# A two-stage attention layer on one core: turned inputs spread over four slots, norm two groups ahead, output row added by VectorE

## What is computed

```python
ln_out = layernorm(hidden_states, ln1_s, ln1_b)
q, k, v = split(ln_out @ w_qkv + b_qkv)
x = hidden_states + merge(attention(q, k, v, ltor_mask)) @ w_ao + b_ao
ln_out = layernorm(x, ln2_s, ln2_b)
q = ln_out @ w_q + b_q
k, v = split(encoder_states @ w_kv + b_kv)
x = x + merge(attention(q, k, v, cross_mask)) @ w_co + b_co
return x + gelu(layernorm(x, ln3_s, ln3_b) @ w1 + b1) @ w2 + b2
# attention: scores * mask - 10000 * (1 - mask), softmax, times v
```

## Time and profile before

| | us |
|---|---|
| runs: median (lowest to highest) | 2038.16 (2036.88 to 2038.91) |
| the profiled execution | 2038.14 |
| its span, first to last instruction | 2036.3 |
| self stage, one group in the loop | about 36.5 |
| cross stage, one group in the loop | about 40.8 |
| MLP, from 1302.8 | 733.5 |

### The profile page before, as it was taken

One profiled execution on the slowest core, in us unless ns is written; L12 is line 12 of the kernel. 1 busy time (PEld: TensorE's weight loads), 2 busy tenths in 40 slices (PEclk: granted clock), 3 DMA queues, 4 the chain that ended last, 5 costly groups with the idle time before them and its releaser, 6 DMA issues. The chain is left out here.

```text
span 2036.3 us, 40263 instructions
## 1 busy us (share of the span) xinstructions
PE 1879.3 (92%) x13328; PEld 1489.4 (73%) x13328; DVE 980.7 (48%) x3338; ACT 1026.6 (50%) x3202; POOL 669.7 (33%) x778
## 2 busy tenths in 40 slices
PE   5999999999988988898889888799999999999999
PEld 4777777777766766676667766588888888888887
DVE  3656566565665556555655565452232323233221
ACT  2666666666666756666666666432222222222222
POOL 2444444444454434344434344440101202020110
PEclk9999999999999999999999999899999999999999
DMA  4311111121121312121112112301010110101010
GB/s 143 106 54 57 44 33 59 41 57 44 33 79 45 112 45 67 44 64 44 61 50 64 44 56 95 135 11 57 6 62 0 62 52 10 52 10 57 5 42 21
DMA packets 71103, 108.07 MB, mean 53 GB/s; under 512 B 12544, under 2 KB 20736, under 8 KB 71040
## 3 DMA queue, kind: packets, MB, share of 16 engines
q1 hardware_dynamic: 71040, 107.27, 16.6%
HBM read 82.07 MB, written 25.17 MB: 53 GB/s over the span
## 5 line engine op out<-in xcount | busy, mean ns | idle before, releaser
L913 POOL TENSOR_TENSOR a_p_s<-a_p_s,a_rcp 128x512 f32<-128x512 f32 x256 | 280.5, 1096 | 679.6 <-DVE a_rcp L759 679.6
L636 ACT ACTIVATE a_p_s<-a_t_s,a_mx 128x128 f32<-128x128 f32 x1024 | 398.8, 395 | 4.9 <-DVE a_mx L750 4.9
L1073 PE MATMUL m_ps_h<-mlp_xT,wt 128*128 128x512 f32 x1536 | 377.3, 396 | 1.8 <-PEq L342 1.8
L1087 PE MATMUL m_ps_y<-m_down_hi,m_g_r 128*128 128x512 f32 x1024 | 343.7, 395 | 0.1
L1073 PEld LDWEIGHTS m_ps_h<-mlp_xT,wt 128*128 128x128 f32 x1536 | 288.0, 188 | 70.9 <-issue 2.0
L1165 DVE TENSOR_TENSOR m_g_r<-m_g_t,m_g_r 128x512 fp32r<-128x512 f32 x128 | 95.3, 745 | 472.8 <-ACT m_g_r L1144 472.8
L740 DVE TENSOR_TENSOR a_ps_s<-a_ps_s,a_m_mul 128x512 f32<-128x512 f32 x256 | 176.7, 690 | 121.6 <-PE a_ps_s L454 119.6
L750 DVE CUSTOM_DVE_ANT_0 a_t_s<-a_ps_s,a_m_add 128x128 f32<-128x128 f32 x1024 | 229.2, 279 | 0.1
L1087 PEld LDWEIGHTS m_ps_y<-m_down_hi,m_g_r 128*128 128x128 f32 x1024 | 192.4, 188 | 44.6 <-issue 0.5
L1128 ACT ACTIVATE m_g_t<-m_ps_h,bias_cols 128x512 f32<-128x512 f32 x128 | 88.1, 689 | 269.5 <-PE m_ps_h L1073 269.3
L496 PE MATMUL a_ps_q<-wt,a_cT 128*128 128x512 f32 x768 | 217.9, 420 | 1.8 <-DVE a_cT L763 1.4
(11 more groups left out here) (78 smaller groups left out, 2544.9 us busy)
## 6 DMA issues: line engine op xcount, KB each, us to landing
a_x_t<-in_x SPq DMA_DIRECT2D x32, 256.0 KB, 2.9
a_res_t<-in_x SPq DMA_DIRECT2D x32, 256.0 KB, 3.1
x_after_self<-a_y_t SPq DMA_DIRECT2D x32, 256.0 KB, 2.0
a_x_t<-x_after_self SPq DMA_DIRECT2D x32, 256.0 KB, 2.8
a_enc_t<-in_ctx SPq DMA_DIRECT2D x32, 256.0 KB, 3.2
a_res_t<-x_after_self SPq DMA_DIRECT2D x32, 256.0 KB, 2.9
raw_wt<-in_w SPq DMA_DIRECT2D x32, 256.0 KB, 4.0
x_after_cross<-a_y_t SPq DMA_DIRECT2D x32, 256.0 KB, 2.0
```

The costliest lines, as they stand in the source:

```text
L636: last = nc.scalar.activation(p_s[:, n % 2, j], t_s[:, n % 2, j], ACT.Exp, scale=-1.0, bias=mx[:, n % 2, j:j + 1], accum_out=sums[:, n % 2 ...
L913: nc.gpsimd.tensor_tensor(p_s[:, n % 2], p_s[:, n % 2], rcp[:, n % 2].unsqueeze(2).to_broadcast([P, HQ, P]), ALU.mult).then_inc(s["normal" ...
L1073: last = nc.tensor.matmul(ps_h[j % 2][:], w1[hw][:, j // KC, kc, (j % KC) * P:(j % KC + 1) * P], xT[:, hx, kc], start=(k == 0), stop=(k == ...
L1087: last = nc.tensor.matmul(ps_y[b][:], g_r[:, j % 2, hg, b * P:(b + 1) * P], w2[hw][:, j // KC, j % KC], start=(j == 0 and x == 0), stop=(j ...
```

## The change

Four things are done.

1. **Turns.** In the cross stage (for groups 17 to 31) TensorE turns x0 in slot 0, x1 and ctx0 in slot 2 and ctx1 in slot 3; between them lie products. For self groups and for group 16 they stay in slots 2 and 3. `flips` lists them for all three engines, those with `last` false ahead of the values' or output's second half. Since `ps_c` is shared, the values of sequence 0 wait for x0's low half.
2. **Norm.** It is made for group g+2 instead of g+1, in slots 5 to 7 instead of 0 to 2: statistics and aggregates in slot 5, centring and first norm in 6, second norm in 7; the inverse roots on GpSimd in slot 5. SP loads x of g+2 in slot 0 instead of 3.
3. **Sums.** In slots 0 and 4 VectorE inverts the sums ahead of scaling the scores; a wait that went with the reciprocal there is kept by a bare semaphore increment, `mask_begun`. GpSimd normalises ahead of preparing the mask.
4. **Output row.** VectorE adds the residual to the output product straight from PSUM, in slots 1 and 4; ScalarE's copy and GpSimd's addition go. TensorE, whose next products use that bank, waits for `y_done` instead of `y_copied`.

```diff
+            def norms_ahead(g):
+                return not isinstance(g, int) or g + 2 <= gN + 1
+
+            def flips(g, n, nxt, last):
+                if not nxt:
+                    at_end = {(gN - 1, 4): (gN, 0), (gN - 1, 5): (gN, 1), (gN, 0): (gN + 1, 0), (gN, 1): (gN + 1, 1)}
+                    return [("x", *at_end[g, n])] if last and (g, n) in at_end else []
+                if not crosses(g + 1):
+                    return [("x", g + 1, n - 2)] if last and n in (2, 3) else []
+                if opens(g + 1):
+                    return [("x", g + 1, n - 2), ("enc", g + 1, n - 2)] if last and n in (2, 3) else []
+                if last:
+                    return [("enc", g + 1, 0)] if n == 2 else []
+                return {0: [("x", g + 1, 0)], 2: [("x", g + 1, 1)], 3: [("enc", g + 1, 1)]}.get(n, [])
...
@@ SP
-                        if n == 3 and (nxt or leads(g + 2 if isinstance(g, int) else 0) and g < gN):
+                        if n == (0 if g != -1 else 2) and norms_ahead(g):
                             load_x(g + 2, 0)
                             load_x(g + 2, 1)
...
@@ TensorE
                         elif known(g, 2):
-                            pe.wait_ge(s["y_copied"], at((g - 1) * GB))
+                            pe.wait_ge(s["y_done"], at((g - 1) * GB))
...
                                 pe.wait_ge(s["k_copied"], at((g + 1) * KC))
+                                if crosses(g) and not (isinstance(g, int) and g == gN - 1):
+                                    pe.wait_ge(s["xTl_done"], at((g + 1) * GB + 1))
...
                         if cur if n >= 3 else prev:
                             weigh_values(*lag(g, n, 3))
+                        for what, k, b in flips(g, n, nxt, False):
+                            (flip_x if what == "x" else flip_enc)(k, b)
                         if n == 0 and prev:
                             outputs(g - 1, 0, 1, cur)
...
@@ ScalarE
-                        if n in (0, 3) and prev:
-                            output_row(g - 1, n // 3)
+                        for what, k, b in flips(g, n, nxt, False):
+                            (flip_x if what == "x" else flip_enc)(k, b)
...
@@ VectorE
+                    def output_row(g, b):
+                        k = g * GB + b + 1
+                        dve.wait_ge(s["res_ready"], at(k))
+                        if known(g, 1):
+                            dve.wait_ge(stored[b], at(16 * g))
+                        dve.wait_ge(s["o_done"], at(k))
+                        nc.vector.tensor_tensor(y_t[:, b], ps_r, res_t[:, b], ALU.add).then_inc(s["y_done"], 1)
...
+                        if n % KC == 0 and (cur if n >= 2 else prev):
+                            invert_sums(*lag(g, n, 2))
                         if cur:
                             scale_scores(g, n)
-                        if n == 2 and ahead:
-                            norm(g + 1, 1)
-                        if n == 0 and ahead:
-                            statistics(g + 1, 0)
-                            statistics(g + 1, 1)
...
+                        if n == 7 and ahead:
+                            norm(g + 2, 1)
+                        if n in (1, 4) and prev:
+                            output_row(g - 1, n // 4)
+                        if n == 5 and ahead:
+                            statistics(g + 2, 0)
+                            statistics(g + 2, 1)
...
+                        if n % KC == 0 and cur and known(g, 1):
+                            dve.wait_ge(s["scaled"], at(slot_no(g, n)))
+                            dve.sem_inc(s["mask_begun"], 1)
+                        if n % KC and (cur if n >= 2 else prev):
...
+                            moments(g + 2, 0)
+                            moments(g + 2, 1)
+                        if n == 6 and ahead:
+                            centre(g + 2, 0)
+                            norm(g + 2, 0)
+                            centre(g + 2, 1)
...
@@ GpSimd
-                    def output_row(g, b):
...
+                        if cur if n >= 2 else prev:
+                            normalise(*lag(g, n, 2))
                         if n == 0 and cur:
                             prepare_mask(g, 1)
                         if n == 7 and nxt:
                             prepare_mask(g + 1, 0)
...
-                        if n == 0 and norms_next(g, cur, nxt):
-                            root(g + 1, 0)
-                            root(g + 1, 1)
+                        if n == 5 and norms_ahead(g):
+                            root(g + 2, 0)
+                            root(g + 2, 1)
...
-                        if n in (1, 4) and prev:
-                            output_row(g - 1, n // 4)
```

More of the change, by code:

```diff
@@ L401, in slot @@
                     def slot(g, n, cur, prev, nxt):
-                        if n == 3 and isinstance(g, int) and g in (NG - 2, gN - 2):
+                        if n == 0 and isinstance(g, int) and g in (NG - 2, gN - 2):
                             for b in range(GB):
@@ L561, in flip_x @@
                         pe.wait_ge(s["xn_done"], at(g * GB + b + 1))
-                        if b == 1 and crosses(g) and not leads(g):
-                            pe.wait_ge(s["encTl_done"], at((g - NG) * GB + b))
-                        elif b == 1 or leads(g) and g > gN:
+                        if b == 1 and opens(g) and crosses(g):
+                            pe.wait_ge(s["encTl_done"], 1)
+                        elif b == 1:
                             pe.wait_ge(s["xTl_done"], at(g * GB + b))
+                        elif leads(g) and g > gN:
+                            pe.wait_ge(s["xTl_done"], g * GB)
+                        elif leads(g) or known(g, 1) and not crosses(g - 1):
+                            pe.wait_ge(s["v_copied"], at((g - 1) * GB + 1))
                         elif known(g, 1):
+                            pe.wait_ge(s["k_copied"], at(g * KC))
+                        if b == 1 and known(g, 1) and crosses(g - 1) and not leads(g):
                             pe.wait_ge(s["v_copied"], at((g - 1) * GB + 1))
@@ L571, in flip_enc @@
                         pe.wait_ge(enc_in[b], at(16 * (g - NG + 1)))
-                        pe.wait_ge(s["xTl_done"], at(g * GB + b + 1))
+                        if opens(g):
+                            pe.wait_ge(s["xTl_done"], g * GB + b + 1)
+                        elif b == 0:
+                            pe.wait_ge(s["xTl_done"], at(g * GB + GB))
+                        else:
+                            pe.wait_ge(s["encTl_done"], at((g - NG) * GB + b))
                         flip(enc_t, b, "encT_done")
@@ L595, in slot @@
                             bias_products(g)
-                        if n in (2, 3) and nxt:
-                            flip_x(g + 1, n - 2)
-                            if crosses(g + 1):
-                                flip_enc(g + 1, n - 2)
+                        for what, k, b in flips(g, n, nxt, True):
+                            (flip_x if what == "x" else flip_enc)(k, b)
                         if n == 3 and cur:
@@ L712, in slot @@
                             split_weights(g, n)
-                        if n in (2, 3) and nxt:
-                            flip_x(g + 1, n - 2)
-                            if crosses(g + 1):
-                                flip_enc(g + 1, n - 2)
+                        for what, k, b in flips(g, n, nxt, True):
+                            (flip_x if what == "x" else flip_enc)(k, b)
                         if not (cur or prev) and n >= 4:
                             split_weights(g, n)
-                        if n in (0, 1, 4, 5) and leads(g):
-                            flip_x(g + n // 4, n % 4)
                     def split_weights(g, n):
@@ L746, in mask_scores @@
                         b, c = divmod(n, KC)
-                        if not known(g, 1) and n < 2:
+                        if not known(g, 1) and (n < 2 or c == 0):
                             dve.wait_ge(s["scaled"], at(slot_no(g, n)))
@@ L826, in slot @@
                             mask_scores(g, n)
[L827 removed]
+                        if n == 5 and ahead:
                             if not cur:
[L829 to L835 removed]
+                                dve.wait_ge(s["stats_done"], (g + 2) * GB + 2)
+                            moments(g + 2, 0)
[4 more added lines that the diff above has]
+                            centre(g + 2, 1)
                         if n == 2 and prev:
```

42 lines of the change are left out of this document (9 added, 33 removed).

## The result

The changed kernel takes 1924.23 us (median of 4 runs, 1923.62 to 1924.77) against 2038.16: ratio 0.9442 [0.9425, 0.9458], 113.9 us less. The profiled execution's span is 1922.6, 113.7 less than before.

A forecast was written before the change was run, and what follows sets the result against it. TensorE, busy 92% of the span, was taken as the bound, so only its waits pay. Self loop 14.0, cross loop 57.8, odd groups and end 19.6 sum to 91.4 us: 2038.1 to 1947, range 1937 to 1982.

The forecast's parts named there:

- Part 1: Cross groups, turns spread over four slots: removes 3.85 us a group, with 0.1 a group taken for a late ctx0 turn.
- Part 2: Norm two groups ahead, sums inverted first: removes 1.17 us a group; new waits 0 in self, 0.1 in cross.
- the chain of 959.3: Slots 6 and 7: estimated sequence from mask and centring through norms and scaling, its normalisation ending at 959.3.
- the shift by 0.4: Slots 5 to 7: output row and four small GpSimd ops delay the normalisation's end by 0.4, to 959.7.
- the forecast's 4.82: Gain per looped cross group, in us: 3.85 from turns plus 1.17 from GpSimd waits, less 0.2 of new waits.
- Part 3: Output row on VectorE, slots 1 and 4: removed copies and additions all off the path, added ops covered; nothing.
- rival B: Cross groups: spread turns not covered, ScalarE stands in exponents; 1.5 a group in 15 groups, 1970 us, chance 0.12.
- The odd groups: Groups 0, 1, 14 to 17, 30 and the end, outside the loops: together 19.6 us won.
- A: Slots 5 to 7: norm's burst collides, TensorE waits for GpSimd there; 1.25 us x 28 groups, 1982 us, chance 0.16.
- C: Slots 5 to 7: collision at its bound plus slow-clocked TensorE, 3.6 a group; slower overall, 2051 us, chance 0.04.
- D: Cross groups: added waits before values hold the spread in step; 3 of 5 us lost each, 1992 us, chance 0.03.
- E: Whole change: every new wait nil and the end worth 6 us; 1937 us, chance 0.05.

The follow-up runs named there:

- The waits put back: Changed kernel plus spare GpSimd additions ahead of slot 1's normalisation, in three sizes: 1927.18, 1936.00 and 1951.29 us.
- the run with the pairs: Changed kernel with the cross stage's turned inputs back in pairs in slots 2 and 3: 1983.77 us, ratio 0.9730.
- the run with the second delay: Changed kernel plus one and a half full-width spare GpSimd additions ahead of slot 1's normalisation: 1936.00 us.

## Why the forecast was too small

Saved by piece, in us of the profiled executions:

| piece | forecast | measured |
|---|---|---|
| self loop, 12 groups | 14.0 | 22.1 |
| cross loop, 12 groups | 57.8 | 73.7 |
| groups 1 and 14 | 1.5 | 2.0 |
| group 0 | 1.6 | 2.2 |
| group 15 | 3 | 3.9 |
| group 16 | 2.5 | 1.7 |
| groups 17 and 30 | 9 | 9.9 |
| end (group 31) | 2 | -1.8 |
| sum | 91.4 | 113.7 |

**The step that failed** is the size of one term, in self and cross: a wait for GpSimd was priced at its shown idle time, 1.17 us a group. It costs 1.84. The forecast had itself read the excess ("about 0.2 us beyond its own length") and used it for the two waits of turns only. Applied to all three waits it gives 0.6 more in each of 24 looped groups, 14 us; as measured, 0.66, it is 16 of the 22.5. The waits put back show the same price from the other side, 0.18 a wait in cross. The rows had it: a self group's idle time was 36.50 - 34.68 = 1.82 in all (the forecast read 1.9), and the change won 1.84 of it with 0.68 still left. And the earlier trace rows show 925.31 - 923.07 = 2.24 for half a product and transposes with a wait of 0.16, against 822.41 - 820.57 = 1.84 after, 0.40 for 0.16.

**Part 1** held. Per cross group the turn of x0 went from 2.25 to 0.41 us (1.84), that of x1 by 1.68, that of ctx1 by 0.14, and scores to keys by 0.38: 4.0 against 3.85, and 4.0 in the run with the pairs. The margin for x0's low half, 0.2 by the forecast, is 822.41 - 822.24 = 0.17, but that it came out so is partly luck: the forecast set 2.5 us of cover against 2.25 of emptying, and both were too long. Measured are 822.41 - 820.16 = 2.25 of cover and 822.24 - 820.16 = 2.08 of emptying. The wait before the turn of ctx0, for which I took 0.1, came: 0.15, without idle time.

**Part 2** held in its result, less in its working. Slots 6 and 7 of a cross group after, VectorE and then GpSimd:

```profile
842.69 0.18 DVE L772 RECIPROCAL a_rcp<-a_sums 128x4 f32<-128x4 f32 x1
...
843.61 0.75 DVE L814 SCALAR_TENSOR_TENSOR a_xn<-a_x_t,a_mv,norm_row 128x512 f32<-128x512 f32 x1
844.40 1.41 DVE L823 SCALAR_TENSOR_TENSOR a_xn<-a_xn,a_rstd,norm_row 128x512 f32<-128x512 f32 x1
845.73 1.77 DVE L814 SCALAR_TENSOR_TENSOR a_xn<-a_x_t,a_mv,norm_row 128x512 f32<-128x512 f32 x1
847.43 0.68 DVE L784 TENSOR_TENSOR a_cT<-a_ps_o,a_cT 128x512 fp32r<-128x512 f32 x1
```
```profile
843.71 1.55 POOL L939 TENSOR_TENSOR a_p_s<-a_p_s,a_rcp 128x512 f32<-128x512 f32 x1
845.22 1.73 POOL L947 TENSOR_TENSOR a_res_t<-a_res_t,bias_row 128x512 f32<-128x512 f32 x1
849.52 1.04 POOL L939 TENSOR_TENSOR a_p_s<-a_p_s,a_rcp 128x512 f32<-128x512 f32 x1 [2.57 <-DVE a_rcp L772]
```

The first centring got in ahead of the normalisation (0.75), and it is the second that ran beside GpSimd, 1.77 in place of the 0.73 I took. The context's low half follows at 847.43, 4.57 before the next scores, 0.2 later than forecast (4.76). Slot 6's reciprocal stands 852.00 - 842.69 = 9.3 us before the next scores, as it did before (960.84 - 951.48), so the two timelines can be laid over each other. The normalisation ends at 850.56, which is 959.4 in the forecast's time: the chain of 959.3 was right, and the shift by 0.4 that was added to it was 0.1. The transposes begin at 851.09, 959.93 in the forecast's time: the 0.3 taken off there for the keys' wait was wrong, since the reciprocal moves up with it. That makes 0.5 of room instead of 0.1 too late. The lengths also bear out the rule cited in the prediction (the Trainium skill, SBUF — State Buffer, Who interferes with whom): 845.22 + 1.73 = 846.95 is the end of GpSimd's op, and 0.55 later, at 847.50, the centring ends.

These account for the cross group. To the forecast's 4.82 come 0.66 for the three waits and 0.19 for the turns (4.04 against 3.85). The new waits cost 0.15 instead of 0.2. And in slot 3 the transposes before stood 940.59 - 938.93 = 1.66 behind their half product, behind a normalisation that ended at 940.54, and stand 834.78 - 833.31 = 1.47 behind it after; from that half product to what follows the transposes it was 2.16 and is 2.00, which gives 0.16 more. Together 5.88 of the 5.92 measured. The remaining 2.6 us of the cross loop are two groups of the profile before, which ran at a granted clock of 0.96 and were longer than the others by 1.5 and 1.1 with the same waits (the first of them, columns as in the earlier trace rows):

```profile
714.36:756.69 42.33, 37.21 (x321) 29.27 (x321) 23.73 (x94) 25.95 (x91) 16.80 (x20) 0.96 0.17 54
```

After, no looped cross group did. The forecast had read one group, without this dip, and multiplied it by 12.

**Part 3** was wrong where it said that the copies and additions are "all off the path". The total doesn't show it, since the change makes all its parts at once, but the output row's copy stood ahead of the cast in ScalarE's queue: left there, with GpSimd's addition, it costs 38.8 us. I had read the margin of slot 0 as a length of work on TensorE, and named rival B's mechanism for exponents only. The price of the added VectorE ops, 0.68, and their cover were right.

**The odd groups.** Group 16 gained less, and the end lost 1.8 instead of winning 2, inside its bounds of -3 and 6. In group 31 TensorE was idle for 18.2 us before, at a granted clock of 0.82, and is idle for 19.6 after, at 0.76. Its waits in group 31 after (1131 to 1189 us):

```profile
PE a_ps_t L476 <- POOL a_p_s L939: 8.9, 4, 3.0
...
PE a_ps_o L488 <- DVE a_cT L784: 2.6, 1, 2.6
```

The norms of two sequences of the last lead meet the split of the MLP's weights there, and a group that is one chain has nothing to cover it. The run that moves these norms on wins 4.1 us in this stretch.

**The rivals.** A and B did not come true in the loops (no wait before transposes in slots 5 to 7, and 0.15 a cross group for the bank); A did in group 31. C did not: the cross group's clock is 1.00. D did not: its sign would be cross groups that keep most of their wait, as in the run with the pairs, and after they keep 0.15. E, at 1937, was the nearest, and lay on the right side for a wrong reason: it took the new waits as nil, and they are 0.15 a cross group, but it put 6 us on the end, which lost 1.8; what was missing came from the price of the old waits.

## What to carry to other kernels

Price a removed wait of TensorE by the distance of the instructions' starts with and without it, not by the idle time shown; of the three short waits here, the part that no idle time shows was a third of the gain. Compare these distances also where no idle time is shown. Before calling an instruction off the path, ask what stands behind it in its queue and what it waits for: an instruction that waits for the end of a product also delays a cast that was ready long before. And parts of a change overlap: norm alone 47 us, row alone 26.5, yet the row is worth 38.8 when it is taken from the full change and the spread of the turns 59.5.

## What was unexpected of the hardware

- A wait of TensorE before its transposes cost a nearly fixed 0.18 to 0.22 us beyond its idle time, at 0.26 as at 0.69 us of idle. It goes by the overlap with the instruction ahead that is lost: 0.16 behind a half product, with 0.06 for the transposes themselves. Behind a turn it was 0.19 (2.25 from turn to turn, 1.65 idle, 0.41 without a wait), behind the scores only 0.08 (1.48 to the keys, 0.30 idle, 1.10 without). The Trainium skill (Perfetto Trace Analysis, Tensor Engine Instruction (MATMUL, LD_WEIGHTS)) says that the profiler computes a matmul's end from its size instead of observing it. That fits an excess booked as busy time; that this is the cause, no run here shows.
- A wait that leaves no idle time in the profile can still cost: 0.10 us a self group in the run with the second delay, 0.15 before the turn of ctx0, 0.23 before slot 3's transposes in self.
- Shortening the end of the cross stage, where TensorE is idle for a third, by 4.1 us lost 2.5 of them again in the 36 matmuls behind it, at a granted clock of 0.73 in place of 1.00; in another run with a stretch as short (53 us) the clock was at 1.00.
